# Another slot order in the second attention of a two-layer recurrence, attention and feed-forward kernel

## The reference

```python
    x = x + _L0_attn_ref(_L0_cond_ref(x, fside_BxSxS_0, fside_BxSxS_0, L0_cond_w, L0_cond_u, cond_512), L0_attn_W, L0_attn_g1, L0_attn_g2, L0_attn_g3)
    x = x + _L0_ffn_ref(_L0_cond2_ref(x, fside_BxSxS_0, fside_BxSxS_0, L0_cond2_w, L0_cond2_u, cond_512), L0_ffn_weight, L0_ffn_bias)
    x = x + _L1_attn_ref(_L1_cond_ref(x, fside_BxSxS_0, fside_BxSxS_0, L1_cond_w, L1_cond_u, cond_512), L1_attn_w_q, L1_attn_w_k, L1_attn_w_v, L1_attn_w_o)
    x = x + _L1_ffn_ref(_L1_cond2_ref(x, fside_BxSxS_0, fside_BxSxS_0, L1_cond2_w, L1_cond2_u, cond_512), L1_ffn_w1, L1_ffn_w2)
```

```python
            def step(carry, x):
                a, b = carry
                ekv_t, ek_t = x
                a = a * decay + ekv_t
                b = b * decay + ek_t
                return ((a, b), (a, b))
...
            num = nf + nb - ekv + euk * vf
            den = df + db - ek + euk
            base = jax.nn.sigmoid(r.astype(jnp.float32)) * (num / jnp.maximum(den, 1e-08))
...
        q = _rope(q)
        k = _rope(k)
        scores = jnp.einsum('bhqd,bhkd->bhqk', q, k) * SCALE
        scores = jnp.where(tok_mask[None, None], scores, -jnp.inf)
        attn = jax.nn.softmax(scores, axis=-1)
        ctx = jnp.einsum('bhqk,bhkd->bhqd', attn, v)
...
        h = _bitlinear(x, w1)
        h = jnp.square(jax.nn.relu(h))
        return _bitlinear(h, w2)
```

## Time and profile before

| what | value |
|---|---|
| median of 3 runs | 345.89 us (344.87 to 347.81) |
| the profiled execution, device time | 342.78 us |
| its span | 341.0 us |
| PE, VectorE, ScalarE, GpSimd busy | 75%, 75%, 60%, 13% of the span |
| mean granted clock of PE | 0.902 |

### The profile page before, as it was taken

One profiled execution on the slowest core, in us unless ns is written; L12 is line 12 of the kernel. 1 busy time (PEld: TensorE's weight loads), 2 busy tenths in 40 slices (PEclk: granted clock), 3 DMA queues, 4 the chain that ended last, 5 costly groups with the idle time before them and its releaser, 6 DMA issues.

```text
span 341.0 us, 6082 instructions
## 1 busy us (share of the span) xinstructions
PE 254.9 (75%) x2321; PEld 161.4 (47%) x2330; DVE 256.7 (75%) x493; ACT 203.1 (60%) x346; POOL 43.8 (13%) x70
## 2 busy tenths in 40 slices
PE   0045395789898889767596959799998888975655
PEld 0024153546465445543354635476566654744423
DVE  1989968979999978969959687963986486565471
ACT  3936749879977968825424676367458444743231
POOL 1202111201112211020124211510020000000000
PEclk9999995979999979999878557958999999997897
DMA  4923633654676663030301444433000010000000
GB/s 122 416 93 62 126 62 71 117 108 79 118 191 126 126 125 62 2 62 0 63 0 33 93 77 86 86 62 63 2 1 2 0 33 0 3 17 15 16 15 31
DMA packets 8524, 23.58 MB, mean 69 GB/s; under 512 B 1584, under 2 KB 2992, under 8 KB 8112
## 3 DMA queue, kind: packets, MB, share of 16 engines
q0 software_dynamic: 4320, 15.73, 24.4%
q1 hardware_dynamic: 4176, 7.48, 6.3%
...
...
## 4 chain that ended last, share of the span: by engine, by line
PE 42%; DVE 30%; issue 11%; DMA 7%; ACT 7%; POOL 3%; DVEq 0%; ACTq 0%; POOLq 0%
PE PS L1374 7%; DVE fwd L723 4%; DMA fwd<-mid 4%; DVE bwd L731 4%; DMA fwd<-bwd 3%; PE PM L1291 3%; PE PO L1389 3%; DVE fwd L1019 3%; PE PO L1164 2%; PE PM L1135 2%; PE PM L1109 2%; PE PM L1219 2%; DVE kp L968 2%; PE PM L1440 2%; PE PO L1188 2%
## 5 line engine op out<-in xcount | busy, mean ns | idle before, releaser
L968 DVE TENSOR_REDUCE kp<-PS 128x2 f32<-128x256 f32 x64 | 32.5, 552 | 23.6 <-PE PS L1353 23.3
L650 ACT ACTIVATE E<-PS 128x384 f32<-128x384 f32 x64 | 27.8, 489 | 26.7 <-PE PS L1374 26.7
L529 ACT ACTIVATE E<-PS,negc,escale 128x1024 f32<-128x1024 f32 x32 | 38.2, 1200 | 5.2 <-PE PS L1149 5.1
L1109 PE MATMUL PM<-w,sg 128*128 128x256 f32 x32 | 11.4, 519 | 25.0 <-DVE sg L746 25.0
L1164 PE MATMUL PO<-E,kp 128*32 128x256 f32 x256 | 20.1, 438 | 5.7 <-DVE ytok L821 3.4
L334 POOL DMA_DIRECT2D fwd<-bwd x15 | 13.1, 872 | 87.7 <-DVE bwd L731 44.5
L1149 PE MATMUL PS<-TP 32*128 32x256 f16 x256 | 20.7, 292 | 4.5 <-DVE TP L773 3.2
L1374 PE MATMUL PS<-TP 32*128 32x256 f32 (+1 forms) x128 | 19.6, 430 | 3.7 <-ACT E L650 3.7
L328 POOL DMA_DIRECT2D fwd<-mid x15 | 13.1, 873 | 65.0 <-DVE fwd L723 64.9
L1109 PEld LDWEIGHTS PM<-w,sg 128*128 128x128 f32 x32 | 7.9, 260 | 27.5 <-DVE sg L746 26.1
L723 DVE TENSOR_TENSOR_SCAN fwd<-DT,ek 128x512 f32<-128x512 f32 x16 | 20.5, 1280 | 0.0
...
## 6 DMA issues: line engine op xcount, KB each, us to landing
fwd<-mid POOLq DMA_DIRECT2D x15, 512.0 KB, 4.6
fwd<-bwd POOLq DMA_DIRECT2D x15, 512.0 KB, 4.5
...
```

Source lines behind the costliest of these rows:

```text
L529: nc.scalar.activation(E[:, p % 6], PS[:, 2 * (p % 2):2 * (p % 2) + 2, :], ACT.Exp, bias=negc[:], scale=escale[:]).then_inc(S["e0_done"], 1)
L650: nc.scalar.activation(E[:, p % 4, i, 0:384], PS[:, i, 0:384], ACT.Exp, scale=QSCALE).then_inc(S["e1_done"], 1)
L968: nc.vector.tensor_reduce(kp[:, b % 2, u * H + 2 * j:u * H + 2 * j + 2, D], PS[:, at0:at0 + 2, lo:hi], AX, ALU.max, negate=True).then_inc( ...
L1109: ins = nc.tensor.matmul(PM[:, 0, u * C:(u + 1) * C], sg[:, seg(b, k * T + u * P, P)], w0[:, 0, k, :], start=(k == 0), stop=(k == HALF - 1))
```

## The change

- `LATE` moves recurrences 12 and 13 one slot later. `wkv` and `gate` of n = 11 go to slots 2 and 3 of their own (they stood with those of n = 12 in slots 4 and 5), and the table load goes to slot -8. The second backward scan now stands ahead of a slot's forward scans.
- The rotary sums of batch 1 move from GpSimd to VectorE. `project_qk`, `rotary` and `gated` of batches 2 and 3 come one slot earlier.
- In the tail `hidden` of tile 5 goes from slot 32 to 34, the turns of tiles 4 and 5 from 33 and 36 to 36 and 37, and some others with them; `project_rows` is split, and the last batch's transposed state comes in slot 33 as `state_rows`. `hidden_q` has a table of its own.

```diff
-        LATE = {BEFORE + 1: (0, 0, 1, 4, 5), BEFORE + 2: (2, 3, 4, 7, 8),
+        LATE = {BEFORE + 1: (1, 1, 2, 5, 6), BEFORE + 2: (3, 4, 5, 8, 9),
                 BEFORE + 3: (5, 6, 7, 10, 11), BEFORE + 4: (8, 9, 10, 13, 14)}
...
-        HID_AT = (17, 19, 25, 27, 31, 32, 38, 39)
-        SQUARE_AT = (17, 19, 25, 27, 31, 32, 38, 39)
-        TURN_AT = (21, 23, 29, 31, 33, 36, 40, 41)
-        DOWN_AT = (22, 24, 30, 32, 34, 38, 40, 41)
+        HID_AT = (17, 19, 25, 27, 31, 34, 38, 39)
+        SQUARE_AT = (17, 19, 25, 27, 33, 34, 38, 39)
+        ROUND_AT = (18, 20, 26, 28, 33, 35, 39, 40)
+        TURN_AT = (21, 23, 29, 31, 36, 37, 40, 41)
+        DOWN_AT = (22, 24, 30, 33, 36, 38, 40, 41)
         PROJ_AT = (13, 21, 28, 35)
+        STATE_AT = (13, 21, 28, 33)
         ROWS_AT = (15, 23, 29, 36)
-        X_AT = (16, 24, 30, 37)
+        X_AT = (16, 24, 30, 38)
         G3_AT = (12, 20, 28, 30)
         TURNY_AT = (11, 19, 27, 34)
-        QK_AT = (-PAIRS, -PAIRS, 0, 1, 7, 8, 15, 16)
-        ROT_AT = (-PAIRS, -PAIRS, 0, 1, 8, 9, 16, 17)
+        QK_AT = (-PAIRS, -PAIRS, 0, 1, 6, 7, 14, 15)
+        ROT_AT = (-PAIRS, -PAIRS, 0, 1, 7, 8, 15, 16)
...
             for p in SLOTS1:
-                for b in range(1, B):
+                for b in range(2, B):
                     if p != ROT_AT[TT * b]:
                         continue
-                    if b >= 2:
-                        pool.wait_ge(S["qre_done"], CH * (b - 1))
+                    pool.wait_ge(S["qre_done"], CH * (b - 1))
                     link(nc.gpsimd.memset(kp[:, b % 2, kq, D:D + 1], 0.0))
                     for u in range(TT):
                         pool.wait_ge(S["rope_done"], TT * b + u + 1)
...
                 for n in steps1(p, 3):
-                    if n == BEFORE + 1:
-                        nc.scalar.preload_act_table_set("natural_log_exp_and_others")
-                        wkv(BEFORE)
                     wkv(n)
+                if p == 2:
+                    wkv(BEFORE)
+                if p == -PAIRS:
+                    nc.scalar.preload_act_table_set("natural_log_exp_and_others")
...
-                if b == 0:
-                    dve.wait_ge(S["rope_done"], u + 1)
-                    dst = kp[:, 0].rearrange("p (n u h) s -> p n u h s", n=2, u=TT)[:, :, u, :, 0:D]
+                if b <= 1:
+                    dve.wait_ge(S["rope_done"], TT * b + u + 1)
+                    dst = kp[:, b].rearrange("p (n u h) s -> p n u h s", n=2, u=TT)[:, :, u, :, 0:D]
                     nc.vector.tensor_tensor(dst, rot1[u].rearrange("p (n h) d -> p n h d", n=2),
                                             rot2[u].rearrange("p (n h) d -> p n h d", n=2),
                                             ALU.add).then_inc(S["qkp_done"], 2)
...
-                for t in tiles(HID_AT, p - 1):
+                for t in tiles(ROUND_AT, p):
                     hidden_q(t)
+                for bb in tiles(X_AT, p):
+                    xqT_copy(bb)
                 for t in tiles(HID_AT, p):
                     relu(t)
                     row_scales(t)
-                for bb in tiles(X_AT, p):
-                    xqT_copy(bb)
...
-                if p in (-2, 5, 13):
-                    gated(2, {-2: 1, 5: 2, 13: 3}[p])
+                if p in (-2, 4, 12):
+                    gated(2, {-2: 1, 4: 2, 12: 3}[p])
+                if p == 3:
+                    gate(BEFORE)
                 for n in steps1(p, 4):
-                    if n == BEFORE + 1:
-                        gate(BEFORE)
                     gate(n)
                 for n in steps1(p, 0):
                     inputs(n)
+                for n in steps1(p, 2, 1):
+                    behind(n, 1)
                 for n in steps1(p, 1):
                     ahead(n, 0)
                 for n in steps1(p, 1, 1):
                     ahead(n, 1)
                 for n in steps1(p, 2):
                     behind(n, 0)
-                for n in steps1(p, 2, 1):
-                    behind(n, 1)
...
-            def project_rows(b):
+            def state_rows(b):
...
                         nc.tensor.matmul(PM[:, 1, at:at + P], xT[:, seg(b, k * T + u * P, P)], ident[:],
                                          start=(u == 0 and k == 0), stop=False, skip_group_check=True)
+
+            def project_rows(b):
                 pe.wait_ge(S["po1_free"], PO1["rows", b] + 1)
...
+                for bb in tiles(STATE_AT, p):
+                    state_rows(bb)
                 for bb in tiles(PROJ_AT, p):
                     project_rows(bb)
```

## The result

| kernel | median | runs | profiled run | span |
|---|---|---|---|---|
| before, beside it | 346.85 us | 4 (344.87 to 348.83) | 342.78 us | 341.0 us |
| changed | 330.8 us | 4 (329.85 to 332.12) | 332.12 us | 330.1 us |

Before's four runs are the three of above and one more. The ratio of the medians is 0.954, interval 0.947 to 0.961: 16 us faster, where I had forecast 8.5 and a range down to 331. In two more measurements, each beside its own runs of before, the changed kernel had 0.957 and 0.965.

The account below looks back on a forecast made before the run. No engine was taken to bound the kernel throughout: waits in the attention and a chain in the tail did. Attention 4.0 plus tail 4.5 gave 8.5 us, so 345.9 - 8.5 = 337.4 us, range 331 to 345.

Parts of the forecast that it names:

- Recurrences 12 and 13 later: Attention slots: moving these recurrences adds no instruction, some 25 us cover the delay; otherwise it would cost 4.2 us.
- Rotary sums of batch 1: Batch 1's turn: PE's 2.87 us wait for GpSimd goes, half counted, less half of VectorE's 0.9 us extra work.
- My reading of the two scans: VectorE at batch 1's sums: 1.74 against 1.21 us shows a scan stretched beside GpSimd, no wait for a whole sum.
- Table load: ScalarE: moving the load and n = 11's pair removes 2.63 of PE's 3.73 us wait; half counted, 1.3 us.
- What the change's profile would show: Expected: table load near 160 us, copy start within 0.3 us, ScalarE's slot 5 transfer wait, PE there under 1.5 us.
- Batch 2 and 3 a slot earlier: Batch 2's turn: PE's 2.16 us wait for GpSimd's sums goes; half counted, 1.1 us.
- Clock: Attention, 186 to 210 us: shorter waits leave PE less time at half clock, worth 0.6 us.
- PE keeps 2.4 GHz: Rival, attention: without waits the clock stays up, 5 us more gained, some 332.5 us; chance 0.17.
- VectorE binds: Rival, attention: PE would only wait elsewhere, so the tail alone counts, 341.4 us; chance 0.20.
- The sign of being wrong that I named: Slots 0 to 12: the prediction is wrong if VectorE has no less idle time than before.
- The tail: After the last values: reordering shortens the chain by 4.5 us, between 1 and 6.
- The slower rival: Slots 5 and 10: ScalarE's transfer wait starves PE, the low clock lasts, 353 us; chance 0.08.

Follow-up runs that it names:

- e11: Kernel before with only recurrences 12 and 13 one slot later and the backward scans ahead of the forward ones in a slot: ratio 0.981.
- e7: Kernel before with only batch 1's rotary sums moved from GpSimd to VectorE: ratio 0.999.
- e4: Changed kernel with the table load and both logarithm and exponential pairs (n = 11 and 12) together again, in slot 5: ratio 0.955, 330.95 us.
- e8: Kernel before with only the query and key products, rotary step and gated input of batches 2 and 3 one slot earlier: ratio 1.011.
- e17: Kernel before with only the tail's tables and order and the later recurrences 12 and 13: ratio 0.960, 330.7 us.
- e6: Changed kernel with the products and rotary step of batches 2 and 3 one slot later again: ratio 0.966, 335.0 us.
- e9: Kernel before with 12 filler products on PE ahead of the turns of batches 1 and 2: ratio 0.998.
- e1: Kernel before with only the tail's tables and order changed: ratio 0.989.
- e5: Changed kernel with recurrences 12 and 13 one slot earlier again: ratio 0.975, 336.8 us.

## Why the prediction was wrong

The direction and both places were right, the size was half. Taken by its own steps:

*Recurrences 12 and 13 later, "No instruction is added".* This step failed: it put the worth of the move at nothing. I asked only who reads the moved results, found 25 us of cover, and wrote zero. The question left out was what had stood behind those instructions on VectorE. It measured 6.8 us alone and 5.8 undone, the largest single term. Two things make it, by the traces: the VectorE instructions of two recurrences, a slot later, let batch 1's rotary products, their sums, the maxima and so PE go ahead (4.3 us up to slot 4 in e11), and on ScalarE load and pairs, a slot later, no longer stand ahead of the exponential that PE needs (3.73 us of waiting became 0.95). In the argument on batch 1's sums I had written that the new order helps VectorE there, and then priced it inside "half of the 2.87".

*Rotary sums of batch 1 (half of 2.87, less 0.45).* Alone 0.999; beside the shift the wait doesn't exist. The doubt "what is late next is VectorE itself" was right, and the half that I took was too much.

My reading of the two scans was wrong. The scan of 1.21 us at 181.57 had GpSimd's sum beside it, and the sum was what took long. VectorE and GpSimd in before, each sum for itself, and a sum of e11 with no scan near:

```profile
181.57 1.21 DVE L723 TENSOR_TENSOR_SCAN fwd<-DT,ekv 128x512 f32<-128x512 f32 x1
181.72 1.57 POOL L384 TENSOR_TENSOR kp<-G 128x256 f32<-128x256 f32 x1 [3.27 <-DVE G L950]
182.70 1.67 DVE L731 TENSOR_TENSOR_SCAN bwd<-ek,DT 128x511 f32<-128x511 f32 x1
183.26 1.63 POOL L384 TENSOR_TENSOR kp<-G 128x256 f32<-128x256 f32 x1
```

```profile
178.26 0.72 POOL L384 TENSOR_TENSOR kp<-G 128x256 f32<-128x256 f32 x1 [10.74 <-DVE G L950]
```

A sum by itself takes 0.72 us. The first one here ends 0.5 us behind the end of the scan that had started before it, the second 0.5 us behind the end of the next, and that scan takes 1.67 us where it has 1.20 alone, as it waited for the first sum. The 1.6 us that I took for a sum's length are a sum and its wait. So the rows agree with the rule of the Trainium skill (SBUF — State Buffer, "SBUF: two separate sides") that the one which comes second waits until the other is through, contrary to what the prediction says of them. In e11 the second sum has a product of 0.75 us ahead of it and not a scan, hence 1.98 instead of 3.17. The waits cost VectorE 0.35 + 0.52 + 0.47 = 1.34 us over batch 1's sums in before (1.10, 1.74 and 1.67 against e7's 0.75, 1.22 and 1.20), so moving the sums, 1.38 us, leaves VectorE's work nearly as it was, where I had put 0.9 us net. Of PE's 2.87 us, 1.19 are the longer sums; the rest is that the second tile's products came late, behind inputs and scan.

*Table load (1.3).* Zero, by e4. In e4 load and pairs stand in slot 5 and the time is that of the changed kernel. What the change's profile would show was right in each point (load at 161.95, copy not delayed, ScalarE waits for the transfer in slot 5, PE under 1.5 us there). What the step left out is the moved pair of n = 11: in slot 2 it stands ahead of the exponential that PE needs next, and PE waits 1.91 us for it, where e4 has 0.63. The switch took 1.28 us again; the copy behind it waited for PE.

*Batch 2 and 3 a slot earlier (1.1).* Alone +1%, beside the shift and the tail zero. The GpSimd wait goes as I wrote; PE then waits for VectorE's maxima (2.56 us in e8, 1.96 in the changed kernel). Undone from the whole it costs 4 us, but e17, which lacks the sums and the load's move too, loses nothing. PE's wait at batch 2's turn is 4.49 us in e6 and 2.91 in e17; in e6 the four sums take 5.1 us, two of them behind scans, in e17 4.2, one of them behind a scan. Which of the two other parts, sums or load, brings this about was not tested.

*Clock (0.6), and the rival "PE keeps 2.4 GHz" (332.5, chance 0.17).* Its time was nearest, its mechanism was not the cause. The clock did rise, 0.79 for 0.51 in those 24 us, but e9 has 0.86 over slots 0 to 12, more than the changed kernel, without a gain in the timed runs. That it rose because PE was better fed fits this; it was not tested by itself. The part of it that makes the low clock a matter of GpSimd's waits fell with e7, where the clock went to 0.50 behind waits of 0.44 and 1.22 us.

*Rival "VectorE binds".* Half right, and I read its sign wrong: VectorE is busy 23.67 of 24 us, but its 46.3 us of work left it 13.0 us idle in slots 0 to 12 of before, and the change, which moves that work about, took 8.2 of these away. The sign of being wrong that I named, no less idle time of VectorE there, did not come.

*The tail (4.5).* Mechanism right, size too small: 6.6 us in the profile. Tanh came 7.2 us after the last values, not 7.9; the turn of x after 11.9, not 12.9; and the relu 2.1 us behind the turn, where I had 3.0 for the missing fillers. Last, tile 6's relu to `final` took 12.5 us instead of 12.8. Alone the tail gave only 1.1% in the medians. In e1's profile slots 12 to 31 were 1.7 us longer than in before and the last leg 1.1 longer (13.9 for 12.8), with the clock at 0.50 from 330 us on; with the shift both are as in before (72.9 and 12.7), and the tail is worth about 2% (0.960 against e11's 0.981, on two chips). Why the clock is lower some 100 us on without the shift is open.

*The slower rival.* ScalarE's wait for transfers came (1.90 us, 5.2 us in three waits up to 237), and PE had no wait behind the first of them, where I had it decide from 3 us on. In e5 the same pair a slot sooner gave 4.09 us, still without making the kernel slower than before.

Looking back, with the shift at 6.8, the tail at 7 and all else at 0, the sum would have been 332 us on the median that I used, against 330.8 measured.
